# A graph attention layer on one core: the first loads shared out anew, part of the statistics on ScalarE, four value slots, and value rows of 576 bytes

## What is computed

```python
h = jnp.maximum(_layernorm(x, axis=-1), 0.0)
x = x + _L0_gnn_ref(h, inlayer2, adj, W, b, w1, b1, w2, b2)

# _L0_gnn_ref(inlayer, inlayer2, adj_mat, ...):
h = inlayer2 @ W.T + b
f1 = h @ w1 + b1
f2 = h @ w2 + b2
logits = f1[:, None] + f2[None, :]
bias_mat = NEG_BIG * (1.0 - (adj_mat > 0).astype(jnp.float32))
coefs = jax.nn.softmax(jax.nn.leaky_relu(logits, LEAKY_SLOPE) + bias_mat, axis=-1)
vals = coefs @ inlayer
```

## Time and profile before

| | us |
|---|---|
| median of 3 runs | 1492.29 (1492.17 to 1492.82) |
| the profiled execution | 1492.2 |
| its span, first to last instruction | 1490.4 |
| TensorE busy | 1425.4 |
| VectorE busy | 1305.4 |
| ScalarE busy | 596.6 |
| GpSimd busy | 265.0 |

### The profile page before, as it was taken

One profiled execution on the slowest core, in us unless ns is written; L12 is line 12 of the kernel. 1 busy time (PEld: TensorE's weight loads), 2 busy tenths in 40 slices (PEclk: granted clock), 3 DMA queues, 4 the chain that ended last, 5 costly groups with the idle time before them and its releaser, 6 DMA issues.

```text
span 1490.4 us, 33313 instructions
## 1 busy us (share of the span) xinstructions
PE 1425.4 (96%) x12585; PEld 1244.2 (83%) x12585; DVE 1305.4 (88%) x1455; ACT 596.6 (40%) x648; POOL 265.0 (18%) x223
## 2 busy tenths in 40 slices
PE   7357999999999999999999999999999999999998
PEld 6235888888888888888888888888888888888887
DVE  5799989898989898989898989898989898989894
ACT  0366434343434343434343434343434343434430
POOL 0275111011101110111011101110111011101111
PEclk9779999999999999999999999999999999999999
DMA  9946999999999999999999999999999999999940
GB/s 299 281 107 150 227 226 210 207 214 207 210 208 214 208 209 208 214 207 208 208 214 208 209 208 214 207 210 207 214 207 211 206 215 207 210 207 214 207 106 10
DMA packets 110164, 302.36 MB, mean 203 GB/s; under 512 B 11716, under 2 KB 44612, under 8 KB 110148
## 3 DMA queue, kind: packets, MB, share of 16 engines
q1 hardware_dynamic: 101296, 293.78, 88.3%
q10 hardware_dynamic: 8852, 8.39, 1.8%
HBM read 293.73 MB, written 8.39 MB: 203 GB/s over the span
## 4 chain that ended last, share of the span: by engine, by line
PE 90%; DVE 4%; SPq 3%; DMA 1%; ACT 1%; issue 1%; POOL 0%; POOLq 0%
PE acc L734 60%; PE acc L736 30%; SPq L259 3%; DMA adj_sb<-in_adj_dram 1%; DVE wgt L567 1%; DVE H L553 1%; DVE stats L499 1%; DVE wT L578 0%; DVE h_mul L543 0%; ACT h_f L384 0%; ACT mask L366 0%; DVE H L551 0%; POOL H L320 0%; SPq L264 0%; DVE b_word L557 0%
## 5 line engine op out<-in xcount | busy, mean ns | idle before, releaser
L734 PE MATMUL acc<-H,wT 128*128 128x257 f16 x8192 | 1367.1, 274 | 44.2 <-DVE wT L578 28.6
L736 PE MATMUL acc<-H,wT 128*128 128x257 f16 x4096 | 1114.7, 272 | 0.0
L734 PEld LDWEIGHTS acc<-H,wT 128*128 128x128 bf16 x8192 | 795.4, 97 | 160.1 <-issue 46.5
L578 DVE STREAM_TRANSPOSE wT<-wgt 128x1024 f32<-128x1024 f32 x512 | 634.4, 1239 | 144.4 <-PE acc L736 144.4
L366 ACT ACTIVATE mask<-adj_sb 128x1024 bf16<-128x1024 int32 x512 | 532.0, 1054 | 541.3 <-DVE wgt L567 495.6
L567 DVE SCALAR_TENSOR_TENSOR wgt<-b_word,c_word,mask 128x1024 f32<-128x1024 f32 x512 | 639.9, 1261 | 6.1 <-ACT mask L366 6.1
L736 PEld LDWEIGHTS acc<-H,wT 128*128 128x128 f16 x4096 | 404.6, 99 | 52.2
L327 POOL TENSOR_TENSOR x_res<-o_raw,x_res 128x256 f32<-128x256 f32 x64 | 64.8, 1013 | 1137.6 <-ACT o_raw L373 1103.0
L373 ACT ACTIVATE o_raw<-acc,r_den 128x256 f32<-128x256 f32 x64 | 30.3, 474 | 282.7 <-DVE r_den L597 282.7
L332 POOL TENSOR_TENSOR o_sb<-o_sb,x_res 128x256 f32<-128x256 f32 x64 | 84.3, 1317 | 5.4
L329 POOL TENSOR_SCALAR o_sb<-h_mean,no_nb 128x256 f32<-128x256 f32 x64 | 58.8, 919 | 0.0
(11 more groups left out here) (70 smaller groups left out, 104.2 us busy)
## 6 DMA issues: line engine op xcount, KB each, us to landing
adj_sb<-in_adj_dram SPq DMA_DIRECT2D x512, 512.0 KB, 8.5
x_res<-in_x_dram SPq DMA_DIRECT2D x64, 128.0 KB, 3.9
out_dram<-o_sb SPq DMA_DIRECT2D x64, 128.0 KB, 4.2
H<-in_x_dram ACTq DMA_DIRECT2D x16, 256.0 KB, 12.3
H<-in_x_dram SPq DMA_DIRECT2D x16, 256.0 KB, 12.7
wgt<-in_L_gnn_inlayer_dram ACTq DMA_DIRECT2D x8, 256.0 KB, 9.5
wgt<-in_L_gnn_inlayer_dram SPq DMA_DIRECT2D x8, 256.0 KB, 10.0
adj_sb<-in_L_gnn_inlayer_dram ACTq DMA_DIRECT2D x8, 256.0 KB, 12.7
```

The costliest lines, as they stand in the source:

```text
L578: nc.vector.transpose(wT[:, k % 4, :, :].rearrange("p t (g r) -> p g t r", g=Q), wgt[:, c, :, s * SQ:(s + 1) * SQ]).then_inc(t_ready, 1)
L734: pe.matmul(acc[:, par, 0:DV], w_hi[:, k % 4, t, :], H[:, j, part, 0:DV], start=(j == 0 and part == 0), stop=False)
L736: mm = pe.matmul(acc[:, par, 0:DV], w_lo[:, k % 4, t, :], H[:, j, 0, 0:DV], start=False, stop=(j == ROWS - 1))
```

## The change

It does four things and what they need:

- The first loads have a new order. SP and ScalarE load `inlayer2` as before (SP quadrants 0 and 1, ScalarE 2 and 3). Of x, SP loads quadrants 0 and 1, woven between: strip 0 behind in2 strip 3, strip 1 behind 4, strips 2 and 3 behind 7, then adjacency chunk 0, x 4 and 5, chunk 1, x 6 and 7. GpSimd's queue loads quadrants 2 and 3 of x and of the first row tile's adjacency; it waits for in2 strips 2, 3, 6 and 7 to land before x strips 0 to 3. Later row tiles are loaded by SP alone, as before.
- Of x strips 0 to 2 (`AS` = 3) ScalarE makes the statistics: a pass with `Copy` and one with `Square` per row tile, each with an accumulated sum, around the copies of f; GpSimd makes the variance of the sum of squares. VectorE keeps strips 3 to 7, strips 5 to 7 in row tile 0.
- Values get a fourth slot (`HR` = 4). It is `o_room`, which joins `o_raw` and `o_sb` and is also what ScalarE's passes write to; `f_rows` moves into the mask's first half.
- `DVP` becomes D + 32 = 288: rows of `H` are 576 bytes apart, of which 514 are read.

```diff
-    DVP = D + 2
+    DVP = D + 32
-    HR = 3
+    HR = 4
+    AS = 3
-        f_rows = sb("f_rows", [P, NCH * CQ], F32)
+        f_rows = mask[:, 0, :].bitcast(F32)
-        o_raw = sb("o_raw", [P, 2, D], F32)
-        o_sb = sb("o_sb", [P, 2, D], F32)
+        o_room = sb("o_room", [P, HALF, D], F32)
+        o_raw = o_room[:, 0:2, :]
+        o_sb = o_room[:, 2:4, :]
+        def h_slot(n):
+            return o_room[:, :, :] if n % HR == HR - 1 else h_f32[:, n % HR, :, :]
...
         @block.sync
-            first_loads(sp, (0, 1))
+            load_in2(sp, 0, 4, (0, 1))
+            load_x(sp, 0, 1, xs_loaded, (0, 1))
+            load_in2(sp, 4, 5, (0, 1))
+            load_x(sp, 1, 2, xs_loaded, (0, 1))
+            load_in2(sp, 5, 8, (0, 1))
+            load_x(sp, 2, 4, xs_loaded, (0, 1))
             sp.wait_ge(in2T_ready, 2 * 6)
-            load_adj(sp, 0, 0)
+            load_adj(sp, 0, 0, adj_loaded[0], (0, 1))
+            load_x(sp, 4, 6, xs_loaded, (0, 1))
             sp.wait_ge(in2T_ready, 2 * 8)
-            load_adj(sp, 0, 1)
+            load_adj(sp, 0, 1, adj_loaded[1], (0, 1))
+            load_x(sp, 6, 8, xs_loaded, (0, 1))
...
         @block.gpsimd
+            for k, ahead in ((0, 2), (1, 3), (2, 6), (3, 7)):
+                pool.wait_ge(in2_loaded[ahead], 64)
+                load_x(pool, k, k + 1, xs_far_loaded, (2, 3))
+            pool.wait_ge(in2T_ready, 2 * 6)
+            load_adj(pool, 0, 0, adj_far_loaded[0], (2, 3))
+            load_x(pool, 4, 6, xs_far_loaded, (2, 3))
+            pool.wait_ge(in2T_ready, 2 * 8)
+            load_adj(pool, 0, 1, adj_far_loaded[1], (2, 3))
+            load_x(pool, 6, 8, xs_far_loaded, (2, 3))
+            def variance_of_squares(k):
+                pool.wait_ge(x_passes, 2 * TS * (k + 1))
+                nc.gpsimd.tensor_scalar(var_eps[:, TS * k:TS * (k + 1)], square_sum[:, TS * k:TS * (k + 1)], 1.0 / D,
+                                        EPS, ALU.mult, ALU.add).then_inc(square_var_ready, 1)
-            for k in range(4):
+            for k in range(AS):
+                variance_of_squares(k)
                 rstds(k)
+            rstds(3)
             for k in range(NS):
                 low_of_values(2 * k)
-                if 1 <= k <= 4:
-                    rstds(k + 3)
+                if k < 4:
+                    rstds(k + 4)
                 low_of_values(2 * k + 1)
...
         @block.scalar
-            first_loads(act, (2, 3))
+            load_in2(act, 0, 8, (2, 3))
             def mask_part(I, g, c):
-                act.wait_ge(adj_loaded[c], 16 * Q * (I + 1))
+                if is_row(I, 0):
+                    act.wait_ge(adj_far_loaded[c], 32)
+                act.wait_ge(adj_loaded[c], 16 * Q * I + 32)
+            def x_pass(n, func, accum, **kw):
+                if n >= HALF:
+                    act.wait_ge(x_passes, n - HALF + 1)
+                k, j = n // (2 * TS), n % TS
+                nc.scalar.activation(o_room[:, n % HALF, :], x_stage(k)[:, j, :], func,
+                                     accum_out=accum[:, TS * k + j:TS * k + j + 1], **kw).then_inc(x_passes, 1)
+            def sums(k):
+                act.wait_ge(xs_loaded[k], 32)
+                act.wait_ge(xs_far_loaded[k], 32)
+                for n in range(2 * TS * k, 2 * TS * k + TS):
+                    x_pass(n, ACT.Copy, x_sum)
+                act.wait_ge(x_passes, 2 * TS * k + TS)
+                nc.scalar.mul(neg_mean[:, TS * k:TS * (k + 1)], x_sum[:, TS * k:TS * (k + 1)],
+                              -1.0 / D).then_inc(neg_mean_ready, 1)
+            def squares(k):
+                act.wait_ge(neg_mean_ready, k + 1)
+                for n in range(2 * TS * k + TS, 2 * TS * (k + 1)):
+                    x_pass(n, ACT.Square, square_sum, bias=neg_mean[:, TS * k + n % TS:TS * k + n % TS + 1])
+            sums(0)
+            squares(0)
             f_to_sbuf(0)
+            sums(1)
+            squares(1)
+            sums(2)
             f_to_sbuf(1)
+            squares(2)
...
         @block.vector
-            for k in range(2, 6):
+            for k in range(2, NS):
                 turn_in2(k)
-            raw_stats(0, 4)
-            turn_in2(6)
-            raw_stats(4, 8)
-            turn_in2(7)
-            mean_var(0)
-            raw_stats(8, 16)
-            mean_var(1)
             chunk_f(0)
-            raw_stats(16, 24)
+            raw_stats(24, 32)
+            mean_var(3)
             chunk_f(1)
-            raw_stats(24, 25)
+            raw_stats(32, 33)
...
-            raw_stats(25, 26)
+            raw_stats(33, 34)
...
-            mean_var(2)
-            raw_stats(26, 32)
+            raw_stats(34, 38)
...
             weights(0, 0, 0)
-            mean_var(3)
+            raw_stats(38, 40)
+            mean_var(4)
...
             affine(2)
+            affine(3)
...
-                        if u < 4:
-                            raw_stats(TS * (u + 4), TS * (u + 4) + HALF)
+                        if u < 3:
+                            raw_stats(TS * (u + 5), TS * (u + 5) + HALF)
...
+                        if u < 3:
+                            raw_stats(TS * (u + 5) + HALF, TS * (u + 6))
+                            mean_var(u + 5)
                         if u < 4:
+                            affine(u + 4)
```

More of the change, by code:

```diff
@@ L95, in graph_attention @@
         r_den = sb("r_den", [P, 2], F32)
[L97 removed]
+        h_f32 = sb("h_f32", [P, HR - 1, HALF, D], F32)
         ident = sb("ident", [P, P], F32)
@@ L112, in graph_attention @@
         var_eps = sb("var_eps", [P, ROWS], F32)
+        x_sum = sb("x_sum", [P, AS * TS], F32)
+        neg_mean = sb("neg_mean", [P, AS * TS], F32)
+        square_sum = sb("square_sum", [P, AS * TS], F32)
         minus_half = sb("minus_half", [P, TS], F32)
@@ L185, in graph_attention @@
         xs_loaded = [sem(f"xs_loaded{i}") for i in range(NS)]
+        xs_far_loaded = [sem(f"xs_far_loaded{i}") for i in range(NS)]
         zeroed = sem("zeroed")
@@ L214, in graph_attention @@
         stats_ready = sem("stats_ready")
+        x_passes = sem("x_passes")
+        neg_mean_ready = sem("neg_mean_ready")
+        square_var_ready = sem("square_var_ready")
         var_ready = sem("var_ready")
@@ L225, in graph_attention @@
         adj_loaded = [sem(f"adj_loaded{c}") for c in range(NCH)]
+        adj_far_loaded = [sem(f"adj_far_loaded{c}") for c in range(NCH)]
         m_ready = sem("m_ready")
@@ L259, in load_strip, with load_adj, load_in2, load_x @@
                 eng.dma_start(stage[B * q:B * (q + 1), :, :], source[k // SC, k % SC, q]).then_inc(signal, 16)
-        def load_adj(eng, I, c):
-            for q in (0, 2, 1, 3):
+        def load_adj(eng, I, c, signal, quadrants=(0, 2, 1, 3)):
+            for q in quadrants:
                 eng.dma_start(adj_sb[B * q:B * (q + 1), c, :].rearrange("r (g n) -> r g n", g=Q),
-                              adj_q[I, c, q]).then_inc(adj_loaded[c], 16)
-        def first_loads(eng, quadrants):
-            for k in range(NS):
+                              adj_q[I, c, q]).then_inc(signal, 16)
+        def load_in2(eng, first, end, quadrants):
+            for k in range(first, end):
                 load_strip(eng, in2_stage(k), in2_q, k, in2_loaded[k], quadrants)
-            for k in range(NS):
-                load_strip(eng, x_stage(k), x_q, k, xs_loaded[k], quadrants)
+        def load_x(eng, first, end, signals, quadrants):
+            for k in range(first, end):
+                load_strip(eng, x_stage(k), x_q, k, signals[k], quadrants)
         @block.sync
@@ L378, in values @@
                 act.wait_ge(h_affine_ready, n // 2 + 1)
+                if n == HR - 1:
+                    act.wait_ge(x_passes, 2 * TS * AS)
                 if n >= HR:
@@ L383, in values @@
                     j = HALF * n + t
-                    nc.scalar.activation(h_f32[:, n % HR, t, :], x_stage(n // 2)[:, j % TS, :], ACT.Relu,
+                    nc.scalar.activation(h_slot(n)[:, t, :], x_stage(n // 2)[:, j % TS, :], ACT.Relu,
                                          scale=h_mul[:, j:j + 1], bias=h_add[:, j:j + 1]).then_inc(h_ready, 1)
+            def x_pass(n, func, accum, **kw):
[18 more added lines that the diff above has]
+            squares(0)
             f_to_sbuf(0)
+            sums(1)
+            squares(1)
+            sums(2)
             f_to_sbuf(1)
+            squares(2)
             act.wait_ge(f_offset_ready, 1)
@@ L497, in raw_stats @@
                     if j == first or j % TS == 0:
-                        dve.wait_ge(xs_loaded[j // TS], 64)
+                        dve.wait_ge(xs_loaded[j // TS], 32)
+                        dve.wait_ge(xs_far_loaded[j // TS], 32)
                     nc.vector.bn_stats(out=stats[:, j, :], in_=x_stage(j // TS)[:, j % TS, :]).then_inc(stats_ready, 1)
@@ L543, in affine @@
                 then_wait(nc.vector.tensor_tensor(h_mul[:, at], rstd[:, at], D_big[:, at], ALU.mult))
```

(21 more changed lines are left out.)

14 lines of the change are left out of this document (8 added, 6 removed).

## The result

The changed kernel takes **1488.31 us** (median of 10 runs, 1487.05 to 1489.69) against 1492.58 for the kernel before: ratio 0.9972, 95% interval 0.9964 to 0.9980. It is 4.3 us faster where 25 were forecast, outside the range. In it L807 and L809 are the products (before L734 and L736), L817 the sums of values, L640 the weights, L651 the turn.

What follows compares the result with a forecast made beforehand. Two limits: loads and VectorE's chain at the start, TensorE's matmuls in the steady part. From 1492.2 us, -16.9 (pitch) - 5.9 (first product) - 2.5 (row tile 0) = -25.3 gave 1466.9 us; range 1458 to 1485.

Steps and rivals of the forecast that it cites:

- The pitch: Steady-part products: 576-byte rows start on multiples of 64, removing some 4.4 ns lost once in three matmuls; -16.9 us.
- all matmuls come down to 109.3 ns: Steady-part products: every matmul takes the short step instead of the mean 110.7 ns, over 12,096 matmuls; -16.9 us.
- The test on L744: Sums of values, f16 weights alone: still 110.7 ns over the same rows, taken as evidence for the address as cause.
- The multiple of 8: Product rows at 516 bytes: part 1 starts 4 past a multiple of 8 bytes, taken to cost the 4.4 ns.
- Rival 1: Products: the pitch does nothing, the 4.4 ns belong to the switch from bf16 to f16 weights; 1483.8 us, chance 0.24.
- The start: Load stage: adjacency lands at 51 us, first weights 5.3 earlier, a wait gone; first product at 75.6, -5.9 us.
- the pair's rate: Adjacency chunk 0 by SP and GpSimd: its 2.1 MB take 6.1 us instead of 8.9, a guess that could be 0.
- GpSimd's issues: GpSimd's 20 DMAs ahead of its first rstd: 1.0 us per issue where 1.25 is allowed, so cost 0.
- Row tile 0: VectorE in row tile 0: one strip without statistics saves at most 3.4 us, limited by GpSimd's work; -2.5 us.
- ScalarE's statistics: Load stage: 48 passes at 0.51 us take 24.7, done by 49 to 50 us, before f_offset; cost 0.
- rival 3: Load stage: GpSimd's issues become the bound; at 3 us each 1508 us, or 1491 with the pitch working; chance 0.04.
- Rival 2: The pitch works, the start isn't shorter: ScalarE's passes over 0.8 us or GpSimd's issues about 1.85; 1475.3 us, chance 0.11.

Runs made afterwards that it cites:

- e2: The kernel before with H rows of 520 bytes (DVP = D + 4) and f_rows in the mask to make room; 1489.89 us in one execution.
- e1: The kernel before with H rows of 576 bytes alone, f_rows laid into the mask to make room; 1484.22 us, ratio 0.9943.
- e9: e7 with GpSimd's queue put back for the far halves of x strips 3 to 7 and adjacency chunk 1; 1481.68 us, ratio 0.9928.
- e7: e1 without GpSimd's queue: SyncE and ScalarE load adjacency chunk 0 behind x strip 2, SyncE the rest; f turned ahead of most statistics; 1479.93 us.
- e4: The changed kernel with far halves of x strips 0 to 3 issued by ScalarE behind its inlayer2 strips instead of GpSimd; 1492.20 us, ratio 0.9995.
- e3: The changed kernel with f's chain ahead of ScalarE's statistics of x strip 2 and VectorE's of strips 3 and 4; 1483.28 us, ratio 0.9939.
- e8: e7 with ScalarE making the statistics of strips 0 and 1, and GpSimd's rstd of strip 3 behind its first low part; 1477.66 us.
- e10: e8 with GpSimd's rstds and low parts reordered and VectorE's affine steps one strip later; 1479.84 us, ratio 0.9911.
- e12: e10 with affine steps back as in e8, GpSimd's rstds from strip 3 moved, ScalarE's fifth mask ahead of strip 1's values; 1475.42 us.

## Why the prediction was wrong

**The sum.** "Faster" was right, and of the 25.3 us of the sum 5.0 came in the profiled execution (4.3 in the medians). The whole miss is 20.3: 11.0 at the first product (-5.9 forecast, +5.1 measured), 7.8 in the pitch, 1.5 in row tile 0.

**The pitch: the long step went, as forecast; its size and its cause were wrong.** The failed step is "all matmuls come down to 109.3 ns". The long step went, as said, but all steps became 110.0: 110.76 - 110.00 = 0.76 ns, over the 11,904 matmuls of 62 tiles the 9.1 measured, where 16.9 were forecast. A uniform step need not be the shortest of the uneven ones. The Trainium skill's floor (TensorE: Matmul & The Clock Gate, "Wait — 56ns, not 53.3ns?") gives 109.6; the measured 110.0 is nearer to it than the 109.3 that I chose, and the sum by it was 13.3. The test on L744 pointed at the address rightly (L817 is flat now, 1.91 us instead of 1.93 for 16). The multiple of 8, which would do for that walk, does not for the products (e2). Rival 1 (the pitch does nothing) is out by e1; its switch of weights may still have a part in the long step, as e2 leaves open.

**The start: the sign was wrong.** The failed step is the loads' rate: four strips fewer ahead of adjacency chunk 0 at 346 GB/s, then "the pair's rate" for SyncE and GpSimd, "a guess that could be 0". I bounded it by no gain, where the range had to hold a loss. Adjacency chunk 0 landed at 59.76, not 51, x strip 4 at 63.25, not 54. The windows and landings show three things: GpSimd's x halves ran against the pair's inlayer2 (284 GB/s between 25 and 30; VectorE waited 4.89 and 4.41 us for strips 4 and 5); between GpSimd's gates SyncE loaded alone (200 GB/s), so GpSimd's last gate opened at 42.4 instead of 37.2; and afterwards the queues shared packet by packet (265, of which SyncE's halves of x got 60). e9 against e7 shows that GpSimd's queue delays the others; e4, which took away the first two, was 3.9 us slower, with x strip 4 at 68.43. How the loss divides among the three is not shown. I priced GpSimd's issues at length, and what its queue does to the others not at all.

**The order around f_offset.** I had seen that a statistic of x strip 4 stands ahead of f_offset and priced the strip at its landing, 54: right step, wrong landing. I had not followed the second copy of f: it stood behind the sums of x strip 2, whose far half landed at 51.31, so it ran at 54.83, where 43.4 was forecast. e3 removes both, and with them 3.6 us.

**From f_offset on.** 6.86 us to the first weights for 6.7 forecast. From there to the first product 15.2 for 13.7: two operations of VectorE took 3.06 and 2.12 us where the same ones took 1.29 and 0.19 in e7 without GpSimd beside them. Both ran while GpSimd made a low part (76.19 to 79.21 and 81.30 to 83.62), and the second ended 1.15 us behind it. This fits the shared port pair of the Trainium skill (SBUF — State Buffer, "SBUF: two separate sides"): whichever of the two engines starts first has it for its whole instruction, and the other waits. The form I had cited, GpSimd kept from issuing DMAs, did not show: 0.54 to 0.60 us for all but the first issue. But while GpSimd issued, VectorE ran transposes and a single short copy (0.21 us), so this is no test of it.

**Row tile 0: -1.0 for -2.5.** VectorE's statistics there shrank from 32 to 24 (11.2 to 8.4 us) with one mean_var less, and the affine steps from 7.3 to 5.2 (four instead of five), but the weights grew from 17.6 to 19.4 and the casts of values from 12.1 to 14.3. GpSimd worked beside them before too; what lengthened them is not shown. Groups of VectorE within row tile 0 of the changed kernel:

```profile
L640 DVE SCALAR_TENSOR_TENSOR wgt<-b_word,c_word,mask 128x1024 f32<-128x1024 f32 x11 | 19.4, 1775 | 0.0
L626 DVE CAST H<-h_f 128x1024 f16<-128x1024 f32 x10 | 11.6, 1165 | 0.0
...
L626 DVE CAST H<-o_room 128x1024 f16<-128x1024 f32 x4 | 2.7, 680 | 0.0
```

**ScalarE's statistics.** 0.40 a sum and 0.50 a square for 0.51 forecast. Their length cost nothing, as said; their place did, ahead of the second copy of f, and they ended at 59.8 instead of 50 for want of x strip 2. GpSimd's issues took 0.58 for 1.0, so rival 3 is out. Rival 2 named a start that isn't shorter, for reasons (passes, issues) that did not hold; none of the rivals had the loads themselves slower, which was the case.

## What to carry to other kernels

A queue added to the loads is not added rate: count packets per queue and bytes per packet, and see whose bytes are wanted first. Here two queues with equal packets moved 346 GB/s, and a third with packets four times as large took the share of the transfers on the critical path. Work moved off a busy engine pays only if the steps that fed it (in-order queues, rstd, affine) keep their distance: e8, e10 and e12 are the same work in three orders, 1475.4 to 1479.8 us.
